# A block of four GNN and mixture-of-experts layers: fewer scatters ahead of a power on GpSimd, and an earlier second scatter in the expert stages

## The reference, cut to what matters

```python
x = x + gat(layernorm(x), adj)          # graph attention
x = x + experts0(layernorm(x))          # 8 experts, hidden 512, top 2, relu
x = x + gru_gnn(layernorm(x), adj)      # 3 steps: m = h @ W[i]; a = A^T m; h = GRU(a, h)
x = x + experts1(layernorm(x))          # 16 experts, hidden 256, top 2, silu(h1) * h2
```

## Time and profile before

| what | value |
|---|---|
| median of 3 runs | 1218.86 us (1217.56 to 1221.72) |
| the profiled execution, its own time | 1222.84 us |
| its span, first to last instruction | 1220.7 us |
| mean granted TensorE clock | 0.891 of full speed |
| busy: PE, PEld, DVE, ACT, POOL | 987.0, 810.6, 770.1, 586.2, 583.4 us |
| scatters on GpSimd, expert stages (L1554) | 280, mean 1001 ns |
| scatters on GpSimd, GRU stage (L394) | 128, mean 1011 ns |

### The profile page before, as it was taken

How to read it: one execution, slowest core, us unless ns; L and a number is a source line. 1 busy time by engine, 2 the same in 40 slices (tenths; PEclk the granted TensorE clock), 3 DMA queues, 4 the chain that set the end, 5 groups by cost and what they waited for, 6 DMA issues and landing times. The chain is left out here.

```text
span 1220.7 us, 28230 instructions
## 1 busy us (share of the span) xinstructions
PE 987.0 (81%) x6880; PEld 810.6 (66%) x6881; DVE 770.1 (63%) x2955; ACT 586.2 (48%) x1485; POOL 583.4 (48%) x622
## 2 busy tenths in 40 slices
PE   4776774499999999199999989889952699999920
PEld 3665663499999999155555555555531699999920
DVE  4667765366666666347878878778663355555527
ACT  3777773233333343046655655556431344444425
POOL 1276677255555555201254263362445267666630
PEclk8778786699999999699999999999985799999965
DMA  9511112222222221222023032040006233333239
GB/s 230 184 49 48 46 50 74 62 72 69 69 69 70 70 70 48 61 68 70 19 87 93 11 103 84 19 146 7 30 27 89 71 96 89 93 89 93 75 110 328
DMA packets 121885, 98.73 MB, mean 81 GB/s; under 512 B 33384, under 2 KB 110824, under 8 KB 121576
## 3 DMA queue, kind: packets, MB, share of 16 engines
q1 hardware_dynamic: 101216, 61.24, 18.6%
q0 software_dynamic: 17152, 35.29, 9.0%
q10 hardware_dynamic: 3464, 1.59, 0.8%
HBM read 55.44 MB, written 42.62 MB: 80 GB/s over the span
## 5 line engine op out<-in xcount | busy, mean ns | idle before, releaser
L1554 POOL DMA_INDIRECT result<-e_y,e_ids x280 | 280.3, 1001 | 221.6 <-DVE e_y L1671 107.7
L1584 PE MATMUL e_ps_h<-e_xT,e_up_of 128*128 128x128 f32 x2240 | 276.9, 278 | 0.0
L1584 PEld LDWEIGHTS e_ps_h<-e_xT,e_up_of 128*128 128x128 f32 x2240 | 265.2, 194 | 0.0
L1599 PE MATMUL e_ps_y<-w_sb,e_hT 128*128 x1664 | 208.3, 275 | 0.0
L1599 PEld LDWEIGHTS e_ps_y<-w_sb,e_hT 128*128 128x128 f32 x1664 | 196.8, 192 | 0.2 <-issue 0.2
L664 POOL DMA_INDIRECT queue<-a_rows,a_slots x128 | 126.6, 989 | 90.4 <-issue 81.1
L394 POOL DMA_INDIRECT queue<-g_q_rows,g_q_slots x128 | 129.5, 1011 | 80.3 <-DVE g_q_gap L327 42.5
L1623 ACT ACTIVATE e_hT<-e_ps_h,b_sb 128x128 f32<-128x128 f32 x272 | 77.5, 368 | 113.3 <-PE e_ps_h L1584 113.3
L1653 DVE COPY e_up_of<-w_sb 128x512 f32 x280 | 114.4, 449 | 3.5 <-issue 0.7
L1679 DVE TENSOR_TENSOR e_hT<-e_ps_h,e_gate 128x512 f32<-128x512 f32 x72 | 49.7, 691 | 84.4 <-ACT e_gate L1632 84.3
L242 POOL TENSOR_TENSOR g_head_rstd<-g_head_vare,half_neg 128x4 f32<-128x4 f32 x16 | 16.3, 1022 | 174.2 <-DVE g_head_vare L235 174.2
(11 more groups left out here) (220 smaller groups left out, 1814.0 us busy)
## 6 DMA issues: line engine op xcount, KB each, us to landing
e_xq<-queue SPq DMA_DIRECT2D x280, 64.5 KB, 1.9
g_y<-result SPq DMA_DIRECT2D x16, 512.0 KB, 4.3
o_y<-result SPq DMA_DIRECT2D x16, 512.0 KB, 5.3
result<-e_y,e_ids POOLq DMA_INDIRECT x280, 2.2
x_res<-x SPq DMA_DIRECT2D x16, 256.0 KB, 3.8
w_sb<-w SPq DMA_DIRECT2D x2, 2048.0 KB, 11.5
w_sb<-w SPq DMA_DIRECT2D x16, 256.0 KB
out<-x_res SPq DMA_DIRECT2D x16, 256.0 KB, 4.5
```

Source lines behind the costliest of these rows:

```text
L1554: pool.indirect_dma_start(out=result, out_offset=bass.IndirectOffsetOnAxis(ap=ids[at_down.k][:, t, :].bitcast(U32), axis=0), in_=y[at_down ...
L1584: last = pe.matmul(ps_h[b][:, t, q * P:(q + 1) * P], up_of[at_up.k % 4][:, t, q * P:(q + 1) * P], xT[at_up.k % 4][:, t, :], start=True, st ...
L1599: last = pe.matmul(ps_y[b][:, t * D:(t + 1) * D], hT[at_down.k % 4][:, t, q * P:(q + 1) * P], down[:, bass.ds(e * (chunks * P) + q * P, P) ...
```

## The change

In the GRU stage one late scatter, not four, stands ahead of the first power of the tail, and seven, not four, between the first and the second. In the expert stages GpSimd no longer waits, ahead of the second scatter of a pair s, until the up products of pair s+3 are made; the waits for y stay. The last three pairs had no such wait before.

```diff
@@ GRU stage, GpSimd's body @@
                 if late:
-                    queue_rows(pool, c, r, VK, AT1, c.queue1, late, 0, 4)
+                    queue_rows(pool, c, r, VK, AT1, c.queue1, late, 0, 1)
                 if has_tail:
                     rstd_and_shift(pool, c, tail_norm, VT, GT, AT0, group(n - 1, 0))
                 if late:
-                    queue_rows(pool, c, r, VK, AT1, c.queue1, late, 4)
+                    queue_rows(pool, c, r, VK, AT1, c.queue1, late, 1)
                 if has_tail:
                     rstd_and_shift(pool, c, tail_norm, VT, GT, AT0, group(n - 1, 1))
@@ expert stages, GpSimd's body @@
                     for t in range(PAIR):
                         pool.wait_ge(y_copied, at_down.s * PAIR + (t + 1))
-                        if t and not (type(at_down.s) is int and at_down.s + down_lag - up_lag + 1 >= pairs):
-                            pool.wait_ge(h_made, at_down.s + (down_lag - up_lag + 2))
                         alone(pool, c)
                         pool.indirect_dma_start(
```

## The result

The changed kernel takes 1233.11 us (median of 4 runs, 1232.29 to 1236.07), the kernel before 1219.98 in the same session (4 runs, 1217.56 to 1221.72): ratio 1.0113, 95% interval 1.0087 to 1.014. It is slower, by some 13 us, and the predicted range ended at 1227.5. The two profiled executions stand 11.1 us apart (1233.92 against 1222.84), and this is the difference that can be taken to pieces.

A forecast was written before the change was run, and what follows sets the result against it. TensorE was taken to bound the expert stages, the order of waits the GRU stage. Steady bodies +0.3, clock +1.4, body 7 -1.0, tail +3.6 and experts -0.4 gave +3.9 us: 1222.8 us, 8-in-10 range 1218.5 to 1227.5.

The forecast's parts named there:

- Which wait binds: GRU bodies: the second wait, for late scatters to land before the second group's ids, sets the body; steady bodies +0.3 us.
- the first gain: At the first tail power, ScalarE starts normalising at v+1.5 instead of v+4.95 (v: end of first tail group's variance), 3.4 us.
- Rival (1): GRU bodies: the second wait doesn't bind, so 3.4 us stay gained in six bodies, 1201.7 us; chance a twentieth.
- Ids at v+12.12: GRU bodies: second tail group's ids written 12.12 us after the first group's variance ends (v), 0.33 later than body 4 before.
- The clock: Bodies 2 to 6: TensorE's lower clock after its pause costs 0.7 us in two of five bodies, +1.4; bounds 0 and 6.5.
- VectorE has work in hand: GRU bodies: the case in which a fall of TensorE's clock costs a body 0 of at most 1.3 us.
- The rival with the clock falling in every body: GRU bodies: TensorE's clock falls in each, +6.5 us of clock, +10 in all, 1229 us; chance 0.07.
- Body 7 and the tail: GRU stage's end: body 7 follows TensorE, -1.0 us; in body 8 the last scatters come later, +3.6, whole on the end.
- The expert stages: Both expert stages: TensorE stays full, dropping the wait gives 0 in the first and -0.4 us at the second's end.
- The sum: Whole kernel: +0.3+1.4-1.0+3.6-0.4=+3.9 us, set on the median 1218.86, giving 1222.8 us.

The follow-up runs named there:

- two and six: Kernel before with two late scatters ahead of the tail's first power and six behind it, instead of four and four: 1225.19 us, ratio 0.9996.
- experiment 4: Kernel before plus four thrown-away TensorE products ahead of the second tail group's transposes, only in bodies with late scatters: 1236.75 us, ratio 1.0129.
- experiment 7: Changed kernel with four and four late scatters again in body 8 alone: 1231.39 us, ratio 1.0077; in the 1346 us session 1365.28, ratio 1.0145.

## Why the prediction was wrong

**Which wait binds: right.** The second landing sets the body, the first gain is taken back whole. The waits moved as forecast (ScalarE's first from about 5 to 2.2 us, its second from under 1 to 4.5), and two and six has no loss in the bodies. ScalarE's first start comes at v+2.0, where v+1.5 was forecast. Rival (1), with a gain of 17 us, did not come: no form of the bodies is more than 2 us shorter than the kernel before.

**Ids at v+12.12: 0.4 to 0.7 us too early, five times.** They come at v+12.80, 12.72, 12.58, 12.70 and 12.52. The count of the instructions was right, their durations were taken from another place in the body. At v the power now runs at once, and the shift and the first scatter behind it fall beside VectorE's state update: 0.67 us instead of 0.20 and 1.41 instead of 1.03 in bodies 2 to 5. Between the two GpSimd stands idle for 0.17 us instead of 0.55, so that together they cost 0.45 us: the last late scatter is at v+10.07, not at the forecast's 9.62. Body 8, where VectorE has no such work at v, has it at v+9.61. What happens can be read from pairs of rows of the changed kernel: in body 6, where the state update starts 1.3 us later, the shift takes 0.20 again; in body 7, where it starts together with the power, the power takes 1.59 instead of 1.04.

```profile
824.16 0.20 POOL L244 TENSOR_TENSOR g_tail_shift<-g_tail_minus_mean,g_tail_rstd 128x4 f32<-128x4 f32 x1
...
824.65 0.69 DVE L1343 TENSOR_TENSOR g_rg<-g_state,g_new 128x512 f32<-128x512 f32 x1
824.91 1.34 POOL L394 DMA_INDIRECT queue<-g_q_rows,g_q_slots  x1 [0.55 <-issue]
...
872.16 0.69 DVE L1343 TENSOR_TENSOR g_rg<-g_state,g_new 128x512 f32<-128x512 f32 x1
872.16 1.59 POOL L242 TENSOR_TENSOR g_tail_rstd<-g_tail_vare,half_neg 128x4 f32<-128x4 f32 x1 [1.06 <-DVE g_tail_vare L235]
```

The Trainium skill (page "SBUF — State Buffer", section "SBUF: two separate sides") says that a VectorE operation with two inputs in SBUF and a GpSimd operation that reads SBUF exclude each other. These rows agree with it, at least in part: in body 4 the shift ends as VectorE's L1345 ends (722.98 and 722.92), and the scatter, begun at 723.15, ends 0.91 us after L1351 has ended (724.56 and 723.65), which is about the 0.96 us of an undisturbed one. But another pair of rows of body 4 does not show the whole instruction blocked: the power runs from 721.20 to 722.24 and L1343, with two inputs in SBUF, from 721.51 to 722.20, both at their ordinary length. That VectorE's work is the cause is read from which rows stand beside each other; no experiment changed it alone. The prediction weighed this rule for the expert stages alone, where it changed nothing, and not at the place to which the edit moved GpSimd's work. In the five bodies the ids come 2.7 us later in sum than forecast (63.32 less 60.6): 2.2 of it is the later last scatter, 0.5 the way from its issue to the ids, 2.50 to 2.73 us where 2.5 was taken.

**The clock: the step that failed.** "VectorE has work in hand" was read from body 4 of the kernel before, in which VectorE waits for nobody behind the ids, and so 0.7 us in two of five bodies was taken. But that body had come out of its pause at the full clock. The change moves the pause to just ahead of the products of the second group, from which agg, new and VectorE's next state update hang with hardly any slack; experiment 4 puts it at 0.2 to 0.4 us. The price could have been read from the kernel before itself: in bodies 2 and 6, where its clock fell, ids to next v took 38.03 and 37.80 us, 1.6 and 1.4 more than 36.41 and twice the 0.7 that was taken. The forecast let these two losses go, by setting 36.41 in all five bodies, and put 1.4 in their place. Measured in place of +1.4: +5.5 (0.5, 1.1, 1.8, 1.9 and 0.2 in the five bodies), close to the upper bound of 6.5. The rival with the clock falling in every body, 1229 with a chance of 0.07, had this part of the mechanism; it had no place for ids later than v+12.12 beside it, and its chance was too small.

**Body 7 and the tail: right.** -0.75 where -1.0, +3.57 where +3.6 was forecast. The agreement of the tail is partly luck: against other executions of the old order it would be 1.5 to 2.8. That it counts in full on the end is not shown by experiment 7.

**The expert stages: right.** No effect; -0.4 could not be told from 0 and, by the spread of the stretch behind the last scatter, is not visible in a trace either. VectorE was not blocked to any effect: in the first expert stretch it is busy for 157.56 us, 157.64 before, with TensorE full in both.

**The sum.** Of the 7.2 us between +3.9 and +11.1, the clock is 4.1, the ids 2.7, and the rest is the scatter between executions.

## What to carry to other kernels

When a stall is moved, price the place where it lands, not the one from which it came: which engine stands still there, at what clock it comes back, and what hangs behind it. That an engine shows no wait in a trace says nothing of how much slack it has; a few thrown-away products put in at that spot measure it, if only bodies at the same clock are compared, and the same products in a real pause show what the clock costs. An engine that is going to wait can do, for nothing, as much of its later work as fits into the wait (here the second scatter: one ahead of the power cost the bodies 8.5 us, two cost none; two were no better than four), and durations for the new place are to be taken from rows with the same neighbours on VectorE.

## What the runs showed of the hardware

- GpSimd's small operations took longer where VectorE operations with two SBUF inputs started before or with them: the shift 0.67 us instead of 0.20, a scatter 1.41 instead of 1.03, the power 1.59 instead of 1.04. Where the power had started 0.31 us ahead of such an operation, neither was longer (1.04 and 0.69).
- After a pause of 2.88 us TensorE came back at the lower clock (1.2 GHz; a mean of 0.58 over seven microseconds), after one of 3.30 us in body 4 of the kernel before it came back at 2.4 GHz (1.00). In body 2 of the kernel before a pause of 2.48 us was followed by the lower clock (1.06 us for four transposes). With 2.83 us of products in the place of the first pause it stayed at 2.4 GHz. In these rows the length of the pause alone does not foretell the clock.
- In one session, on chip 1, the kernel before took 1346 us instead of about 1222 on chips 3 and 12, ten per cent more; whether it was the chip or the session is open. The ratios moved too: a gain of 1.1% measured there was 0.24% elsewhere.
